# Mamba mixer, head of the scan: the last two convolution tiles finished inside the scan by tanh, chunk 0's outputs issued first

## The reference, cut to what matters

```
zxbcdt = layernorm(x) @ in_proj_w.T            # z 512, xBC 640, dt 4 columns
dt  = softplus(dt + dt_bias)
xBC = silu(causal depthwise conv of xBC, 4 taps, + conv_b)
xs, B, C = xBC                                 # xs: 4 heads x 128
y   = scan over tokens of (xs*dt, A*dt, B, C) + xs * D
g   = y * silu(z);  g = g * rsqrt(mean(g*g)) * norm_w
x   = x + g @ out_proj_w.T
```

## Time and profile before

| | us |
|---|---|
| three runs, lowest, median, highest | 528.64, 529.23, 529.54 |
| the profiled execution, its own time | 529.58 |
| its span in the profile | 527.8 |
| busy in the span: PE, DVE, ACT, POOL | 506.1, 410.0, 312.7, 145.7 |

### The profile page before, as it was taken

The page is one execution under the profiler, slowest core; times in us unless marked ns, Lnnn a source line. Parts: engine busy times, 40 slices in busy tenths (PEclk is TensorE's granted clock), DMA queues, the critical chain, the costliest instruction groups (busy, mean ns, idle before and its releaser), DMA issues.

```text
span 527.8 us, 9002 instructions
## 1 busy us (share of the span) xinstructions
PE 506.1 (96%) x2939; PEld 427.1 (81%) x2939; DVE 410.0 (78%) x900; ACT 312.7 (59%) x783; POOL 145.7 (28%) x285
## 2 busy tenths in 40 slices
PE   5999999999999999999999999989988999999996
PEld 4778899999999987678888888758877768888884
DVE  5626567667675898899998999965886779899777
ACT  3656878688687754665443445998762355443342
POOL 2241425344243320110110302379434120020110
PEclk9999999999999999999999999999999999999999
DMA  7320100000001303000040000000000000000101
GB/s 281 105 95 1 36 7 2 2 0 2 2 2 25 131 2 140 6 1 0 1 140 1 2 0 1 1 1 2 0 2 0 1 1 1 1 0 1 40 2 40
DMA packets 5789, 14.23 MB, mean 27 GB/s; under 512 B 624, under 2 KB 2928, under 8 KB 5744
## 3 DMA queue, kind: packets, MB, share of 16 engines
q1 hardware_dynamic: 5744, 13.67, 7.4%
HBM read 12.62 MB, written 1.05 MB: 26 GB/s over the span
## 4 chain that ended last, share of the span: by engine, by line
PE 67%; DVE 19%; issue 6%; ACT 5%; POOL 2%; DMA 1%; DVEq 0%; ACTq 0%; POOLq 0%
PE psum L172 55%; PE psum L475 4%; DVE xs L1973 2%; PE psum L507 2%; DVE ln_stats L212 2%; DVE f_t L1296 1%; DVE xn L232 1%; PE psum L240 1%; DVE f_ch L1365 1%; DVE f_ch_hl L1379 1%; DVE xT_hl L254 1%; POOL ln_rstd L226 1%; DVE f_mix L1374 1%; ACT f_sil L1182 1%; PE psum L468 1%
## 5 line engine op out<-in xcount | busy, mean ns | idle before, releaser
L172 PE MATMUL psum<-xT_hl,ffn_w_hl 128*128 128x512 f32 x312 | 77.7, 396 | 0.9 <-ACT f_sil L1182 0.6
L172 PE MATMUL psum<-f_um,ffn_w_hl 128*128 128x512 f32 x288 | 72.9, 399 | 1.1 <-DVE f_t L1296 0.6
L172 PEld LDWEIGHTS psum<-xT_hl,ffn_w_hl 128*128 128x128 f32 x312 | 56.4, 189 | 13.3 <-DVE ffn_w_hl L897 1.4
L172 PEld LDWEIGHTS psum<-f_um,ffn_w_hl 128*128 128x128 f32 x288 | 53.1, 188 | 15.0 <-DVE f_um L1308 1.7
L1182 ACT ACTIVATE f_sil<-psum 128x512 f32<-128x512 f32 (+1 forms) x48 | 28.1, 596 | 48.8 <-PE psum L172 48.8
L1206 ACT ACTIVATE f_ch_hl<-f_ch 128x512 fp32r<-128x512 f32 x48 | 30.4, 632 | 42.2 <-DVE f_ch L1365 40.5
L172 PE MATMUL psum<-xT_hl,wq_hl 128*128 128x512 f32 x192 | 52.0, 407 | 0.6 <-ACT qT L574 0.6
L172 PE MATMUL psum<-wo_hl,oT_hl 128*128 128x256 f32 x384 | 50.8, 281 | 1.0 <-DVE oT_hl L707 0.6
L172 PEld LDWEIGHTS psum<-wo_hl,oT_hl 128*128 128x128 f32 x384 | 47.8, 188 | 3.7 <-DVE oT_hl L707 1.1
L574 ACT ACTIVATE qT<-psum 128x512 f32<-128x512 f32 x32 | 35.3, 1104 | 22.5 <-PE psum L172 22.4
L583 ACT ACTIVATE probs<-probs,small 120x66 f32<-120x66 f32 x120 | 39.8, 338 | 8.2 <-DVE small L684 8.2
(11 more groups left out here) (265 smaller groups left out, 1152.4 us busy)
## 6 DMA issues: line engine op xcount, KB each, us to landing
w_raw<-in_wq SPq DMA_DIRECT2D x4, 512.0 KB, 4.4
w_raw<-in_wo SPq DMA_DIRECT2D x4, 512.0 KB, 3.3
ffn_w_raw<-in_ffn SPq DMA_DIRECT2D x3, 576.0 KB, 4.9
ffn_w_raw_far<-in_ffn SPq DMA_DIRECT2D x3, 576.0 KB, 5.0
ssd_w_raw<-in_ssd SPq DMA_DIRECT2D x3, 512.0 KB, 5.4
x_resid<-in_x SPq DMA_DIRECT2D x2, 512.0 KB, 4.5
out_x<-x_resid SPq DMA_DIRECT2D x4, 256.0 KB, 2.1
w_raw<-in_wk SPq DMA_DIRECT2D x1, 512.0 KB, 6.6
```

Source lines behind the costliest of these rows:

```text
L172: i = e.matmul(dst, lhs(a), rhs(b), start=start and n == 0, stop=stop and n == len(TERMS) - 1, **kw)
```

## The change

1. Tiles 8 and 9 get taps, bias and carry times 0.5 (prepared on POOL), so that the convolution gives h = x/2, and silu(x) = h * (1 + tanh(h)). ACT does the tanh (L1887 of the changed kernel), DVE the rest (`late_silu`, L2048), both inside the scan: tile 8 in chunk 0, tile 9 in chunk 1.
2. ACT's table load therefore comes after silu of tile 7. In chunk 0 ACT does the second exp ahead of `b_tok`.
3. Chunk 0's `x_dt` is one DVE instruction (L2053) behind the last convolution tap instead of four on ACT.
4. PE does outputs(0) ahead of decays(1), with 11 fillers instead of 17; outputs(0) waits for `w_mix` and no longer for `c_exp`.
5. POOL does the `make_xd` of tile 3 after chunk 0's `x_dt_decay`, and takes over `w_lo_conv` from DVE.

```diff
@@ end of the feed-forward layer, dve then pool
                 early(phase, "w_lo_z", e)
                 lora_mask(1)
-                early(phase, "w_lo_conv", e)
                 add(1, 0, 1)
...
                 zeros(1, 1)
                 stacked_rows(1)
+                early(phase, "w_lo_conv", e)
@@ pe
                     if c == 0:
                         e.wait_ge(S["ipz"], len(others))
+                        keep_busy(4, 6)
+                        e.wait_ge(S["sl"], NC - len(LATE))
+                        keep_busy(5, 6)
+                        e.wait_ge(S["L"], 1)
+                        keep_busy(2, 6)
+
+                def outputs(c):
+
+                    if c == 0:
                         conv_done(e, NC - 1)
-                        keep_busy(4, 6)
-                        e.wait_ge(S["sl"], NC)
-                        keep_busy(7, 6)
-                        e.wait_ge(S["L"], 1)
-                        keep_busy(6, 6)
-
-                def outputs(c):
-
-                    e.wait_ge(S["ce"], c + 1)
-                    if c:
+                        e.wait_ge(S["wt"], 1)
+                    else:
+                        e.wait_ge(S["ce"], c + 1)
                         e.wait_ge(S["st"], c)
                         e.wait_ge(S["y"], c)
                     e.wait_ge(S["X"], c + 1)
...
                 for i in range(NT + 3):
+                    if i == 1:
+                        outputs(0)
                     if i < NT:
                         decays(i)
...
-                    if 1 <= i <= NT:
+                    if 2 <= i <= NT:
                         outputs(i - 1)
@@ act
+                def tanh(i):
+                    b, h = order[convs[i]]
+                    conv_done(e, i)
+                    e.wait_ge(S["join"], CONVS.index(b) + 1)
+                    e.activation(th[LATE.index(i)], dst(b)[:, half(h)], ACT.Tanh).then_inc(S["sl"], 1)
...
                 silu_z(19)
-                for i in range(7, NC):
-                    silu(i)
+                silu(7)
...
                         if c == 0:
-                            e.wait_ge(S["dt_pool"], DT_DONE)
...
-                        if c == 0:
+                            e.activation(bank(1), bank(1), ACT.Exp).then_inc(S["L"], 1)
+                            e.activation(btok[:, 0, :], bank(2)[:, P:2 * P], ACT.Copy).then_inc(S["bt"], 1)
+                            tanh(LATE[0])
                             e.wait_ge(S["cm"], 3)
                             e.activation(DA, DA, ACT.Exp).then_inc(S["da"], 1)
+                        else:
...
+                            m.then_inc(S["X"], 1)
+                            if c == 1:
+                                tanh(LATE[1])
@@ dve
+                def late_silu(i):
+
+                    b, h = order[convs[i]]
+                    e.wait_ge(S["sl"], i + 1)
+                    part = dst(b)[:, half(h)]
+                    e.scalar_tensor_tensor(out=part, in0=th[LATE.index(i)], scalar=1.0, in1=part, op0=ALU.add,
+                                           op1=ALU.mult).then_inc(S["slt"], 1)
+
+                e.wait_ge(S["xt"], 1)
+                e.wait_ge(S["dt_pool"], DT_DONE)
+                e.tensor_tensor(xd[0], bank(3).rearrange("p (h l) -> p h l", h=NH), spread(DT[:, 0:NH], P),
+                                ALU.mult).then_inc(S["X"], 1)
                 for i in range(NT + 4):
...
                         e.tensor_tensor(ce[c % 2], bank(1).rearrange("p (h l) -> p h l", h=NH),
                                         repeat(bcT[:, 1, tile(c)], NH), ALU.mult).then_inc(S["ce"], 1)
+                        if c < len(LATE):
+                            late_silu(LATE[c])
@@ pool
-                for i in range(2, NH + 1):
-                    join(i)
+                join(2)
                 make_xd(2)
-                make_xd(3)
+                join(3)
+                join(4)
...
+                    if c == 0:
+                        make_xd(3)
                     if c < NH - 1:
                         make_xd(NC // 2 + 1 + c)
```

More of the change, by code:

```diff
@@ L1560, in mixer @@
             ce, st, gy = (pair(n) for n in ("c_exp", "state", "gated"))
+            th = [at(f"tanh{n}", [P, HALF], F32, slots[o])[:, :] for n, o in enumerate((2, 1))]
             g2 = [at(f"gated_sq{n}", [P, NH, P], F32, slots.pop(0))[:, :, :] for n in range(2)]
@@ L1577, in mixer @@
             dst = lambda b: cb_pre[:, :] if b == 0 else xs[:, b - 2, :]
-            names = ("xda cs cm rhs mb sel gs da raw wh wl bcz ip tap ipz part join cv sl xd dt dt_dve dt_pool dt_act de L G xt X xdd wt ce Y St st1 st y g ghi glo g2 ss "
+            names = ("slt xda cs cm rhs made sel gs da raw wh wl bcz ip tap ipz part join cv sl xd dt dt_dve dt_pool dt_act de L G xt X xdd wt ce Y St st1 st y g ghi glo g2 ss "
                      "ve ri O fin bt").split()
@@ L1626, in mixer @@
             W_ORDER = ("0", "out", "z", "c")
-            WL_ORDER = ("out", "0", "dt", "z", "c")
+            WL_ORDER = ("out", "0", "dt", "z")
             def w_hi0(e):
@@ L1767, in decays @@
                         e.wait_ge(S["X"], c)
+                    if c == HT:
+                        e.wait_ge(S["slt"], len(LATE))
                     for h in range(NH):
@@ L1843, in last_tap @@
                         e.activation(halo[:, b, :], bank(IN_BANK[n])[:, HALF - TAPS:HALF], ACT.Copy)
-                    tap = PR_CW + CONV * b + CONV - 1
-                    e.activation(dst(b)[:, half(h)], bank(IN_BANK[n]), ACT.Identity, scale=par[:, tap:tap + 1],
-                                 bias=par[:, PR_CB + b:PR_CB + b + 1]).then_inc(S["tap"], 1)
+                    i = convs.index(n)
+                    if i == LATE[0]:
+                        e.wait_ge(S["part"], 1)
+                    bias = half_bias[:, b - LATE_B:b - LATE_B + 1] if i in LATE else par[:, PR_CB + b:PR_CB + b + 1]
+                    e.activation(dst(b)[:, half(h)], bank(IN_BANK[n]), ACT.Identity, scale=tap_of(i, CONV - 1),
+                                 bias=bias).then_inc(S["tap"], 1)
                 def dt_copy(n):
@@ L1968, in conv @@
                         out = dst(b)[:, half(h)]
-                        tap = par[:, PR_CW + CONV * b + CONV - 1 - d:PR_CW + CONV * b + CONV - d]
+                        tap = tap_of(i, CONV - 1 - d)
                         e.wait_ge(S["tap"], i + 1)
@@ L2109, in join @@
                     conv_done(e, NC // 2 + i)
-                    e.wait_ge(S["part"], 3 if b == 0 else 6)
+                    e.wait_ge(S["part"], 4 if b == 0 else 8)
                     e.tensor_tensor(out, out, carry[:, b, :], ALU.add).then_inc(S["join"], 1)
```

61 lines of the change are left out of this document (43 added, 18 removed).

## The result

The changed kernel took 533.16 us in the median of six executions (531.47 to 533.57), the kernel before 529.31 us (528.64 to 529.82) in its six: a ratio of 1.0068, 95% interval 1.0053 to 1.0083. It is slower. The forecast was 531.3 us, in a range that ended at 532.4: the direction was right, the size was not, and the time lies above the range. The profiled execution of the changed kernel took 533.57 us, its span 531.8 us (before: 529.58 and 527.8). Those 4.0 us are what I account for first.

The account below looks back on a forecast made before the run. The prediction took PE as the bound, busy 28.94 of 29.00 us from 363 to 392 us. It added 1.42 (head) and 0.67 (f0), 2.09, to 529.23, giving 531.3 us, range 528.3 to 532.4.

Parts of the forecast that it names:

- ACT's part of the head: Scan's head: earlier table load brings the first exp 1.41 us earlier, of which only 0.89 arrive at w_mix.
- PE's part: Scan's head: with outputs(0) ahead, decays(1) comes 0.18 us later and decays(2) 0.10 later, PE waiting about 1.6 between.
- The faster rival: Scan's head: outputs(0) is out of the way when c_exp is ready, decays(1) 0.9 us earlier, 528.3 us; chance 0.20.
- The late silu: Chunk 1, tile 9: DVE's silu, held by POOL's x_dt_decay, ends at 360.56, delaying gated, outputs(1) and decays(3).
- The term of 1.42: Scan's head: decays(3) moves from 363.44 to 364.86, +1.42 us, because outputs(1) waits for gated.
- one hold by DVE: POOL's make_xd of tile 3 and chunk 0's other run from 353.5 to about 357.1, held once by DVE.
- costed at nothing: Small POOL operations, tile 8's tanh and late silu, and POOL's make_xd work fit in existing waits, adding 0.
- The end of f0: POOL's w_lo_conv holds DVE's f_dd additions, so PE's adapter product starts 0.67 us later; bounds 0 and 0.9.
- The milder rival: Engines do not hold each other: f0 term 0, gate term 0.97, 530.2 us; chance 0.24.
- The sum of 2.09: Whole kernel: 1.42 at the scan's head plus 0.67 at the end of f0, giving 531.3 us; chance 0.46.
- The two terms: The +1.42 us at decays(3) in the scan's head and the +0.67 us at the end of f0.
- TensorE's clock falls: Two new PE waits of about 1.6 us between 357 and 362 lower the clock, 533.0 us; chance 0.10.

Follow-up runs that it names:

- e4_decays_first: Changed kernel with w_lo_conv back on DVE, tile 9's late silu behind the first gated, and decays(1) ahead of outputs(0) again: 528.34 us, ratio 0.9982.
- the two kernels with fillers: The changed kernel and the kernel before, each with filler matmuls ahead of the scan's last three projections: 530.92 us (ratio 1.0031) and 529.0 us (ratio 0.9988).
- e1_wlo_on_dve: Changed kernel with only w_lo_conv put back on DVE: 532.81 us, ratio 1.0062.
- after_again: The changed kernel run again unaltered, twelve runs and a second profile: 531.43 us, ratio 1.0038.
- order_alone: Changed kernel with only the order put back, decays(1) ahead of outputs(0): 531.07 us, ratio 1.0025.
- before_delay: Kernel before with 20 filler matmuls ahead of decays(2): 534.16 us, ratio 1.0086.
- after: The changed kernel in its first profile, against the kernel before: profiled execution 533.57 us, median of six 533.16 us, ratio 1.0068.
- e3_both: Changed kernel with w_lo_conv back on DVE and tile 9's late silu behind the first gated: 530.37 us, ratio 1.0018.
- decays_first_fillers: Changed kernel with w_lo_conv on DVE, tile 9's late silu behind gated, decays(1) ahead of outputs(0), fillers before the last three projections: 527.68 us, ratio 0.9969.
- e2_gate_after_gated: Changed kernel with only tile 9's late silu moved behind the first gated: 531.66 us, ratio 1.0035.

## Why the prediction was wrong, step by step

- **ACT's part of the head: right.** Reckoned from decays(0), the first exp is at 3.19 instead of 4.63 (1.44 earlier, forecast 1.41) and `w_mix` at 4.50 instead of 5.43 (0.93, forecast 0.89).
- **PE's part: right.** L1771 of decays(1) is +0.18 and of decays(2) +0.11 (forecast +0.18, +0.10). PE waits 1.50 between them. The faster rival ("outputs(0) is out of the way by the time `c_exp` is ready") fell as its rows said. In e4_decays_first the time is near its price, 528.34 where 528.3 stood, but with the other order and with the silu and the subtraction moved back as well.
- **The late silu: right.** Put 0.99 later for the delay ahead of it, the forecast has the late silu end at 361.55, `gated` at 362.76 and L1771 of decays(3) at 365.85; they came at 361.56, 362.76 and 365.96. The term of 1.42 measured 1.53. The silu ends 0.56 behind the end of POOL's operation, where the forecast had 0.55: DVE waited for POOL here. The Trainium skill's page "SBUF — State Buffer", section "SBUF: two separate sides", says that a DVE operation with two SBUF inputs and a GpSimd operation that reads SBUF exclude each other for the whole instruction, and in this pair the trace agrees. In another it does not: the late silu of tile 8, with the same two SBUF inputs, starts 0.75 us into POOL's `xs_D` and takes 0.68 us, and POOL's two `xs_D` take 3.10 together, as unheld ones do. So the "one hold by DVE" that the forecast put there, under what it costed at nothing, did not come.
- **The end of f0: right.** 0.60 to 0.79 in six profiles, 0.67 forecast. The milder rival fell with it.
- **The sum of 2.09 as the whole change of the time: here it failed.** The two terms themselves measured 2.27 in the first profile (0.74 + 1.53) and 2.09 between the two kernels with fillers (0.60 + 1.49). The step that failed is that all else was put at nothing: the forecast took the 3.4 us at half rate of the earlier trace rows for a fixed part of the kernel, and the start for fixed too. In the first profile the rest behind decays(3) is 1.48 longer and the start 0.25 later. The rest costs 1.0 more at 0.997 than with a full clock and 2.6 more at 0.989, and which of them a run gets changes from run to run (0.989 or 0.990 in 11 of 101 runs of the kernel before, 4 of 18 of the changed one, 4 of 5 of e1_wlo_on_dve, none of 12 of e4_decays_first).
- **The rival "TensorE's clock falls": a near number by luck.** Its 533.0 is near the measured 533.16, but it put the fall to the waits between 357 and 362. In this profile the clock stays at 1.00 there and falls for longer in the tail, where the kernel before has a fall already.
- **Not explained: the median.** The longer fall and the start account for what the profiled execution has beyond the two terms, but not for the median of six. Only two of the six runs are at 0.989. The four at 0.997 took 531.47, 532.48, 533.12 and 533.20, three of them above the range. None of these four has a profile. The one of after_again, at 0.997, is above before's by head and f0 (2.22) and by the start (0.71); whether the start does the same in these is open.
- **Not seen: the scatter of the start.** It differs by up to 1.1 us between executions.
- **Expected, shown in another place.** That waits in the head can pull the clock down did happen, in order_alone.

What stays open: what decides whether the clock falls for 3.4 or for 10 us, and whether the changed kernel draws the long fall more often than the kernel before. 4 of 18 against 11 of 101 does not settle it, and before_delay shows only that a shift alone did not bring it in five runs. What the profiles do show is where the fall begins: 38.1 to 38.5 us behind the second matmul of decays(3) in the three with a long one (after, e1_wlo_on_dve, e3_both), 42.0 to 43.9 us behind it in the seven with 3.4 us in the tail. The groups of after_again (530.5 and 532.2 to 533.0 at the same mean clock) have no profile of the lower one. The start explains up to 1.1 of the 2 us between them; where a 3.4 us fall lies, in the tail or in the head as in order_alone, could be the rest, which is only argued.

## What to carry to other kernels

An operation of DVE that waited for one of POOL and a matmul group taken out of the hole that it filled made a head slower whose first exp came 1.4 us earlier: for every operation moved ahead, ask what it used to hide and what stands behind it in its new queue. A shortened gate shows the next one (0.90 came back where 1.42 was expected, and 1.34 in the other order); undo parts in different orders before giving each a price. And where the profile shows a stretch of half clock, do not treat its length as fixed, since it changes from run to run: put its other lengths into the range, or fill PE's waits first and measure then.

## What the runs showed of the hardware

- Twelve filler matmuls (eighteen in one kernel) in waits of 0.3 to 1.5 us kept TensorE's granted clock at 0.999 or 1.000, in 45 of 45 runs; without them it was at 1.2 GHz for about 3.4 or about 10 us of the scan's tail in each profile, in order_alone for 3.4 us of the head as well.
- PE's first matmuls run slower for a time that changes between executions. The program's first fillers (one line's 16 matmuls: ns min/median/max), before and decays_first_fillers, each with the row of the start behind it:

```profile
L417 PE MATMUL psum<-const_f x16: 379/380/792, 4.9 to 12.5; 128*128 128x256 f32 x16
...
17.05 1.04 PE L240 MATMUL psum<-const_f,xn 128*128 128x128 f32 x8
```

```profile
L417 PE MATMUL psum<-const_f x16: 379/631/796, 5.0 to 13.6; 128*128 128x256 f32 x16
...
18.02 1.04 PE L240 MATMUL psum<-const_f,xn 128*128 128x128 f32 x8
```

  The same matmuls take 380 ns in the median in one and 631 ns in the other, and the start follows, 0.97 us later. The granted clock of these windows reads 1.00 in both, but that is no measurement: the trace's first record of the clock, a step to full rate, lies at 10.6 us in before and at 12.9 us in decays_first_fillers, and there the single matmuls step from 631 to 380 ns. Over all fourteen profiles the first record lies between 9.0 and 12.9 us and the start between 16.96 and 18.02. That the clock is at its lower level ahead of the record is inferred from the durations.
- DVE is not held by every operation of POOL. The late silu, with two SBUF inputs, ends 0.55 us behind POOL's `x_dt_decay` (two inputs) wherever it starts inside one, in eight profiles. Started 0.75 us into POOL's `xs_D` (one input) it takes its 0.68 us, in all ten profiles that have it; started 0.31 us into one it takes 0.91 to 0.92 us (e4_decays_first, decays_first_fillers).
- POOL is held as well: its `xs_D` takes 1.56 us alone and 2.00 us where the late silu of DVE still runs as it starts (361.12 in e2_gate_after_gated, with the silu from 360.90 to 361.69).
